# A two-layer attention and ternary-FFN kernel on one core: FFN statistics a step later, small work moved between engines, and the last output products reordered

## What is computed

```python
xn = layernorm(x)
x = x + attention(xn) + ffn(xn)
```

## Time and profile before

| | us |
|---|---|
| median of 3 runs | 380.17 (379.9 to 381.06) |
| the profiled execution | 380.05 |
| its span, first to last instruction | 378.2 |
| PE busy | 360.5 (95%) |
| DVE busy | 307.1 (81%) |
| POOL busy | 282.3 (75%) |
| ACT busy | 250.7 (66%) |

### The profile page before, as it was taken

The page is one execution under the profiler, slowest core; times in us unless marked ns, Lnnn a source line. Parts: engine busy times, 40 slices in busy tenths (PEclk is TensorE's granted clock), DMA queues, the critical chain, the costliest instruction groups (busy, mean ns, idle before and its releaser), DMA issues.

```text
span 378.2 us, 8305 instructions
## 1 busy us (share of the span) xinstructions
PE 360.5 (95%) x2808; PEld 335.7 (89%) x2824; DVE 307.1 (81%) x684; ACT 250.7 (66%) x804; POOL 282.3 (75%) x242
## 2 busy tenths in 40 slices
PE   8999988997899999999999999999999999999995
PEld 3668878997898999999999999999999999998984
DVE  6868998866999987879878887887787878888882
ACT  1367865563987666777767586867666777767771
POOL 5537759789999999999779697777987977775000
PEclk9999999999999999999999999999999999999999
DMA  7997001523343445343345743343455433334100
GB/s 258 412 409 314 28 30 45 144 66 83 85 109 97 118 118 149 101 121 87 83 114 143 178 114 103 102 105 85 126 136 162 122 85 85 84 100 105 50 2 28
DMA packets 35371, 46.19 MB, mean 122 GB/s; under 512 B 4609, under 2 KB 27138, under 8 KB 34946
## 3 DMA queue, kind: packets, MB, share of 16 engines
q1 hardware_dynamic: 35184, 45.66, 41.8%
q10 hardware_dynamic: 146, 0.00, 0.0%
HBM read 13.14 MB, written 1.05 MB: 38 GB/s over the span
## 4 chain that ended last, share of the span: by engine, by line
PE 80%; DVE 11%; ACT 4%; DMA 2%; issue 2%; POOL 0%; SPq 0%
PE bank L1321 17%; PE bank L1033 13%; PE bank L1341 12%; PE bank L1229 12%; PE bank L1281 10%; PE bank L1188 3%; PE bank L1287 3%; PE bank L1284 2%; ACT bank L519 2%; PE bank L1164 2%; PE bank L1042 2%; DMA wq0T<-in_L_attn_w_qkv_dram 2%; PE bank L1245 2%; DVE neg_max L940 1%; PE bank L1050 1%
## 5 line engine op out<-in xcount | busy, mean ns | idle before, releaser
L519 ACT ACTIVATE bank<-bank,neg_max 128x256 f32<-128x256 f32 (+1 forms) x256 | 101.1, 396 | 10.5 <-DVE neg_max L940 10.3
L528 ACT ACTIVATE probT_hi<-bank 128x512 fp32r<-128x512 f32 x96 | 57.7, 602 | 65.0 <-PE bank L1033 64.9
L940 DVE TENSOR_REDUCE neg_max<-bank 128x2 f32<-128x512 f32 (+1 forms) x96 | 65.9, 687 | 23.6 <-PE bank L1287 13.2
L1321 PE MATMUL bank<-probT_hi,v 128*128 128x256 f32 x384 | 76.5, 295 | 0.7 <-DVE oT_lo L968 0.7
L956 DVE TENSOR_TENSOR prob<-bank,rsum 128x512 f32<-128x512 f32 x96 | 66.4, 691 | 3.3
L962 DVE TENSOR_TENSOR probT_lo<-bank,probT_hi 128x512 fp32r<-128x512 f32 x96 | 65.3, 681 | 0.5 <-ACT probT_hi L528 0.4
L681 POOL TENSOR_TENSOR rope_b<-turned,cst 128x512 f32<-128x512 f32 x36 | 46.9, 1302 | 22.1 <-DMA turned<-raw 22.1
L1281 PE MATMUL bank<-kT,qT 128*128 128x256 f32 (+1 forms) x384 | 62.6, 272 | 0.0
L1033 PE MATMUL bank<-cst,prob 128*128 128x128 f32 x384 | 57.9, 273 | 4.3 <-DVE prob L956 3.3
L1321 PEld LDWEIGHTS bank<-probT_hi,v 128*128 128x128 f32 x384 | 58.7, 189 | 3.6 <-issue 2.3
L1281 PEld LDWEIGHTS bank<-kT,qT 128*128 128x128 f32 x384 | 55.0, 191 | 0.0
(11 more groups left out here) (163 smaller groups left out, 781.7 us busy)
## 6 DMA issues: line engine op xcount, KB each, us to landing
turned<-raw SPq DMA_DIRECT2D x72, 128.0 KB, 2.0
qT<-q_hi SPq DMA_DIRECT2D x64, 128.0 KB, 2.4
qT<-split_lo SPq DMA_DIRECT2D x64, 128.0 KB, 2.4
wq0T<-in_L_attn_w_qkv_dram SPq DMA_DIRECT2D x4, 512.0 KB, 7.9
wout<-in_L_attn_w_out_dram SPq DMA_DIRECT2D x4, 512.0 KB, 12.7
nat_qkv<-in_L_attn_w_qkv_dram SPq DMA_DIRECT2D x2, 1024.0 KB, 20.4
nat_o<-in_L_attn_w_o_dram SPq DMA_DIRECT2D x1, 2048.0 KB, 21.1
kT<-split_hi SPq DMA_DIRECT2D x16, 128.0 KB, 2.4
```

The source lines that it names most:

```text
L519: ins = nc.scalar.activation(own, own, ACT.Exp, bias=neg_max[it % 2][:, first + j:first + j + 1], accum_out=sums[it % 2][:, first + j:firs ...
L528: nc.scalar.activation(probT[0][:, n % 4, :], bank[2 + n % 2][:, :], ACT.Copy).then_inc(t_hi, 1)
L940: dve.tensor_reduce(neg_max[n // UNITS % 2][:, unit_columns(n % UNITS)], score_bank(n)[:, :].rearrange("p (h k) -> p h k", h=heads), AX.X, ...
L1321: ins = pe.matmul(group_bank(), v[b % 2][:, DH * z:DH * z + P], p, start=m == 0, stop=m == last)
```

## The change

- **Layer 0.** `m_products(3)` on PE moves ahead of the wait for `prob0` and its transposes. The four `high_part` copies move from DVE to ACT, two before the exponential and two after the signs of `ffn0`.
- **Tokens of batches 0 and 1.** ACT writes only the even tile of `y1`, POOL the odd one, right after `batch_root` of that batch; `turn_tokens` waits for both.
- **DVE's small products.** In `stats1`, `hidden_scale` and `hidden_stats` a `tensor_tensor` or `scalar_tensor_tensor` of two SBUF inputs becomes a `tensor_scalar` of one column (one for each of the two tiles where there are two). `hidden_scale(0)` moves behind `tokens_lo(0)`.
- **FFN statistics.** `hidden_stats(0)` leaves its place before the loop. `hidden_stats(t)` now runs in step t+1 instead of step t, after `hidden_lo(t)` and ahead of `hidden_factors(t-1)`; for the last tile it runs after `ffn_add(6)`.
- **Signs of the projection.** Two instructions of half the size in ACT's step 1, one before `gelu(1)` and one after the fill's copy, instead of one at the end of step 0. `proj(0)` and `column_sums` wait for both.
- **`mean_part`** moves from DVE (one instruction, slots 6 to 13) to POOL (two instructions, after blocks 10, 12, ... 24).
- **The end.** Slot 97 makes only the e = 0 half of `project_out(15, 0)`. After the last slot come its e = 1 half, then the e = 0 half of `project_out(15, 1)`, then its e = 1 half into bank 6 instead of bank 5. DVE adds bank 5 to both halves, then bank 6 to half 1; SP stores half 0 after the first addition, half 1 after the second.

```diff
 # SP
             sp.wait_ge(out_added, B)
-            sp.dma_start(rows[:, B - 1, :, :], x[:, B - 1, :, :]).then_inc(stored, 16)
-            sp.wait_ge(stored, 16 * B)
+            sp.dma_start(rows[:, B - 1, 0, :], x[:, B - 1, 0, :]).then_inc(stored, 16)
+            sp.wait_ge(last_added, 1)
+            sp.dma_start(rows[:, B - 1, 1, :], x[:, B - 1, 1, :]).then_inc(stored, 16)
+            sp.wait_ge(stored, 16 * (B + 1))
...
 # ACT
             whole_x(2)
+            high_part(0)
+            high_part(1)
             act.wait_ge(e_in, 1)
...
             sign(0, nat_ffn0[:, :, :], ffn0T[:, :, :], tern0)
+            high_part(2)
+            high_part(3)
...
             def normal1(b):
                 act.wait_ge(nb_done, b + 1)
-                for t in (2 * b, 2 * b + 1):
-                    ins = nc.scalar.activation(y1[:, b, t % 2, :], x[:, b, t % 2, :], ACT.Identity, bias=tok[:, 3, t:t + 1],
-                                               scale=tok[:, 0, t:t + 1])
-                ins.then_inc(y1_done, 1)
+                t = 2 * b
+                nc.scalar.activation(y1[:, b, 0, :], x[:, b, 0, :], ACT.Identity, bias=tok[:, 3, t:t + 1],
+                                     scale=tok[:, 0, t:t + 1]).then_inc(y1_even, 1)
...
                 hidden_hi(step - 1, 1)
+                if step == 1:
+                    sign(2, nat_proj[:, 0:4, :], projT[:, 0:4, :], tern_proj)
                 if step < TILES:
                     gelu(step)
                 if step < B - 1:
                     tokens_hi(step + 1)
                 empty(FILLS_IN.get(step, ()))
-                if step == 0:
-                    sign(2, nat_proj[:, :, :], projT[:, :, :], tern_proj)
+                if step == 1:
+                    sign(2, nat_proj[:, 4:8, :], projT[:, 4:8, :], tern_proj)
...
 # POOL
             def normal1(b):
-                for t in (2 * b, 2 * b + 1):
+                for e in range(0 if b >= 2 else 1, 2):
...
             batch_root(0)
+            normal1(0)
             batch_root(1)
+            normal1(1)
...
+            def mean_part(t):
+                if t == 0:
+                    pool.wait_ge(wcol_done, 1)
+                pool.wait_ge(f_add, t + 1)
+                pool.wait_ge(f_norm, t + 1)
+                part, share = x[:, t // 2, t % 2, :], mean_out[:, :]
+                pool.tensor_scalar(share, wcol[:, :], ffac[:, t, 4:5], None, ALU.mult).then_inc(f_share, 1)
+                pool.wait_ge(f_share, t + 1)
+                pool.tensor_tensor(part, part, share, ALU.add).then_inc(f_mean, 1)
...
                 weights_lo(min(n + 6, len(W_UNITS)), min(n + 7, len(W_UNITS)))
+                if n >= 10 and n % 2 == 0 and n < 10 + 2 * TILES:
+                    mean_part((n - 10) // 2)
...
 # DVE
             def hidden_scale(b):
                 link(dve.reciprocal(f1[:, own], ms[:, own]))
-                link(dve.tensor_tensor(f1[:, own], f1[:, own], ms[:, own], ALU.mult))
-                dve.scalar_tensor_tensor(ffac[:, own, 0], c[:, own], wscale[:, 1:2], f1[:, own], ALU.mult, ALU.mult).then_inc(f_fac, 1)
+                for t in (2 * b, 2 * b + 1):
+                    ins = dve.tensor_scalar(f1[:, t:t + 1], f1[:, t:t + 1], ms[:, t:t + 1], None, ALU.mult)
+                link(ins)
+                for t in (2 * b, 2 * b + 1):
+                    ins = dve.tensor_scalar(ffac[:, t, 0:1], c[:, t:t + 1], wscale[:, 1:2], f1[:, t:t + 1], ALU.mult, ALU.mult)
+                ins.then_inc(f_fac, 1)
...
             stats1(1)
-            hidden_scale(0)
             add0(2)
             tokens_lo(0)
+            hidden_scale(0)
             add0(3)
...
             stats1(3)
-            hidden_stats(0)
             hidden_scale(1)
             for step in range(1, STEPS):
                 t = step - 1
...
                 if step in (1, 2):
                     tokens_lo(step + 1)
-                if step < TILES:
-                    hidden_stats(step)
+                if t < TILES - 1:
+                    hidden_stats(t)
                 if t >= 1:
                     hidden_factors(t - 1)
                     ffn_add(t - 1)
+                if t == TILES - 1:
+                    hidden_stats(t)
...
             def slot(n):
-                if 6 <= n < 6 + TILES:
-                    mean_part(n - 6)
...
             add_out(B - 1)
+            dve.wait_ge(out_last, 1)
+            dve.wait_ge(out_added, B)
+            dst = x[:, B - 1, 1, :]
+            dve.tensor_tensor(dst, dst, bank[BANK_LAST][:, DIM:2 * DIM], ALU.add).then_inc(last_added, 1)
...
 # PE
             def turn_tokens(b):
                 pe.wait_ge(y1_done, b + 1)
+                if b < 2:
+                    pe.wait_ge(y1_even, b + 1)
...
+            m_products(3)
             pe.wait_ge(prob0, 1)
...
-            m_products(3)
             ffn_0(0)
...
-                if it and u in (1, 5):
+                if it == ITS and u == 1:
+                    project_out(it - 1, 0, (0,))
+                elif it and u in (1, 5):
                     project_out(it - 1, u // 5)
...
-            project_out(ITS - 1, 1)
+            project_out(ITS - 1, 0, (1,))
+            project_out(ITS - 1, 1, (0,))
+            emptied(pe, FILL[-1])
+            project_out(ITS - 1, 1, (1,), BANK_LAST)
```

More of the change, by code:

```diff
@@ L435, in whole_x, with high_part @@
                 ins.then_inc(full_done, 1)
+            def high_part(b):
+                act.wait_ge(full_done, b + 1)
+                nc.scalar.activation(xT[0][:, :, SEQ * b:SEQ * b + SEQ],
+                                     yT_full[:, b, :].rearrange("p (k t) -> p k t", k=KC), ACT.Copy).then_inc(x_hi, 1)
             keys_x(0)
@@ L649, in normal1 @@
                 pool.wait_ge(nb_done, b + 1)
[L650 to L651 removed]
+                for e in range(0 if b >= 2 else 1, 2):
+                    t = 2 * b + e
+                    ins = pool.tensor_scalar(y1[:, b, e, :], x[:, b, e, :], tok[:, 0, t:t + 1], tok[:, 3, t:t + 1],
                                              ALU.mult, ALU.add)
@@ L833, in _ @@
             ins.then_inc(prob0, 1)
-            for b in range(1, B):
-                high_part(b)
             def weight_scale(n, ps):
@@ L859, in stats1 @@
                 link(dve.reciprocal(ms[:, own], r[:, own]))
-                link(dve.tensor_tensor(ms[:, own], ms[:, own], var[:, own], ALU.mult))
+                for t in (2 * b, 2 * b + 1):
+                    ins = dve.tensor_scalar(ms[:, t:t + 1], ms[:, t:t + 1], var[:, t:t + 1], None, ALU.mult)
+                link(ins)
                 dve.tensor_scalar(tok[:, 3, own], mean[:, own], -1.0, None, ALU.mult)
@@ L902, in hidden_stats @@
                 link(dve.reciprocal(ffac[:, t, 2:3], fv))
-                link(dve.tensor_tensor(ffac[:, t, 2:3], ffac[:, t, 2:3], fv, ALU.mult))
+                link(dve.tensor_scalar(ffac[:, t, 2:3], ffac[:, t, 2:3], fv, None, ALU.mult))
             def hidden_factors(t):
@@ L975, in add_out @@
                 dve.tensor_tensor(dst, dst, bank[BANK_OUT][:, :].rearrange("p (e n) -> p e n", e=2), ALU.add).then_inc(out_added, 1)
-            def mean_part(t):
-                if t == 0:
-                    dve.wait_ge(wcol_done, 1)
-                dve.wait_ge(f_add, t + 1)
-                part = x[:, t // 2, t % 2, :]
-                dve.scalar_tensor_tensor(part, wcol[:, :], ffac[:, t, 4:5], part, ALU.mult, ALU.add).then_inc(f_mean, 1)
             def slot(n):
-                if 6 <= n < 6 + TILES:
-                    mean_part(n - 6)
                 if n % (HKV * UNITS) == UNITS and n > HKV * UNITS:
@@ L1323, in heads_out, with project_out @@
                 ins.then_inc(pv_done, 1)
-            def project_out(it, half):
+            def project_out(it, half, parts=(0, 1), place=BANK_OUT):
                 b, g = of_batch(it)
@@ L1335, in project_out @@
                     pe.wait_ge(w_lo, W_AT["woT", 2 * g + half] + 1)
-                for e in range(2):
+                for e in parts:
                     for s, w in W:
                         for j in (2 * half, 2 * half + 1):
-                            first = g == 0 and half == 0 and e == 0 and (s, w) == (0, 0) and j == 0
+                            first = place == BANK_LAST or (g == 0 and half == 0 and e == 0)
+                            first = first and (s, w) == (0, 0) and j == 2 * half
                             final = g == HKV - 1 and half == 1 and e == 1 and (s, w) == (0, 1) and j == 3
-                            ins = pe.matmul(bank[BANK_OUT][:, DIM * e:DIM * e + DIM], oT[s][:, j, e:e + 2 * P - 1:2],
+                            ins = pe.matmul(bank[place][:, DIM * e:DIM * e + DIM], oT[s][:, j, e:e + 2 * P - 1:2],
                                             woT[w][:, 4 * g + j, :], start=first, stop=final, skip_group_check=True)
                 if g == HKV - 1 and half == 1:
-                    ins.then_inc(out_full, 1)
```

(1 more changed line is left out.)

19 lines of the change are left out of this document (10 added, 9 removed).

## The result

The kernel after takes 382.91 us (median of 5 runs, 382.55 to 383.49), the kernel before 380.16 us (5 runs, 379.79 to 381.06). The ratio is 1.0073, 95% interval 1.0059 to 1.0087: slower by more than the 0.3% set as the bound, and outside the range. The profiled execution has a span of 380.7 us against 378.2, at a granted clock of 0.995 against 0.999.

A forecast was written before the change was run, and what follows sets the result against it. PE sets the pace from 120 to 340 us, with POOL as full at 120 to 145 and behind. Front 0, mean products 0, end -0.5: 380.05 becomes 379.5 us, range 377.2 to 381.1.

The forecast's parts named there:

- rival 3: Block 9 lands later still through POOL's late root of tile 6: slot 21 later, 380.8 to 381.4 us; chance 0.10.
- Rival 4: The wait at slot 21 halves PE's clock for one slot, costing up to 2.85 us: 382.4 us; chance 0.05.
- rival 1: POOL isn't the bound: the front's 3.4 us arrive and PE's stalls in slots 6 to 13 shrink, 375.4 us; chance 0.18.
- Layer 0, 1.2 us earlier: Before fc(0): the 0.66 us gap goes and sharing y1 saves 0.55, so fc(0) starts 1.2 us earlier.
- DVE's stretch, 1.65 us beyond that: From tokens_lo(0) to tile 0's addition: fewer statistics and unheld small products, 2.8 us earlier including layer 0's 1.2.
- 1.0 us back: In DVE's stretch: hidden_scale, held 1.22 us instead of 0.22 behind POOL, gets 1.0 us back as one-column tensor_scalar.
- PE to step 8, 0.6 us out of the wait: Ahead of proj(6): DVE no longer waits for gelu(7), 0.6 us less; PE reaches the slots 3.4 us early.
- The request for the root of tile 6, 81.9: DVE asks POOL for this root at 81.9 instead of 79.27, so POOL starts it 2.6 us late.
- POOL's lateness: POOL 2.3 us late from 85.58 on, 1.0 at block 8 after 1.3 us come back from mean_part.
- Slot 21, 150.2: Block 9 lands at 150.0, slot 21 starts at 150.1 to 150.2; the front's gain becomes a 3 us wait.
- The mean products, 1.3 us: On POOL after block 10 and later: 1.3 us for two instructions, the other seven (9 us) fit in at 0.
- The end, 0.5: Last addition and store are half as large: 0.27 + 0.23 = 0.5 us less, between 0.27 and 0.7.

The follow-up runs named there:

- run 3: The changed kernel with POOL's order alone changed, each root of a hidden tile one piece of RoPE work later: 376.22 us, ratio 0.9896.
- run 12: The changed kernel with POOL's roots one piece of RoPE later and the mean's share back on DVE: 377.57 us, ratio 0.9924.
- run 11: The kernel before with two layer 0 edits alone (high parts on ACT, m_products(3) ahead of the transposes): 380.47 us, ratio 1.0002.
- run 5: The changed kernel with the high parts of x back on DVE: 383.49 us, ratio 1.0086.
- S: Part of the change: FFN statistics one step later, projection's signs in two halves; alone on the kernel before 383.99 us.
- run 4: The kernel before with only the FFN statistics one step later and the projection's signs in two halves: 383.99 us, ratio 1.0104.
- run 1: The changed kernel with the FFN statistics and the projection's signs back in their old places: 379.73 us, ratio 0.9988.
- run 6: The changed kernel with the mean's share back on DVE, one instruction instead of two on POOL: 385.3 us, ratio 1.0130.
- run 2: The changed kernel with fifteen idle products on PE ahead of slot 21's wait: 382.5 us, ratio 1.0063.
- run 7: The kernel before with the change of its end alone: 379.47 us, ratio 0.9986.
- run 9: The kernel before with POOL's order alone changed, each root one piece of RoPE later: 383.12 us, ratio 1.0073.
- run 10: The kernel before with FFN statistics one step later, signs in two halves, and POOL's roots one piece of RoPE later: 377.86 us, ratio 0.9930.

## Why the prediction was wrong, step by step

**The sign, and what decided.** Forecast 379.5; what came is rivals 3 and 4 in one, 0.15 of the chances together. The mechanism of the sum held: POOL is late by its roots, block 9 lands late, and slot 21 eats the front's gain. With POOL's order put right (run 3) the kernel takes 376.22, near rival 1's 375.4, though by other terms: PE is 2.1 us early after the FFN (93.07 for 95.17) and not 3.4, and the mean off DVE gives 1.3 (run 12) and not 0.8. What failed are terms of the sum, two of which were put at nothing: the clock, and the later mean products on POOL.

**Layer 0, 1.2 us earlier: measured none.** This is the first step that failed, as "DVE loses its copies, which ACT takes where it otherwise waits" and "the gap of 0.66 us ahead of the transposes goes". Counted from the start of PE's products `bank<-g,xrT`, `fc(0)` starts after 18.82 us before and 18.88 after. The gap went elsewhere, for two reasons. The first is what the copies do on ACT: they stand ahead of its table load, and they let POOL start sooner. Neither was counted. ACT's timeline of the kernel after, with L446 the copies of batches 2 and 3:

```profile
26.82 1.14 ACT L446 ACTIVATE xT_hi<-yT_full 128x512 fp32r<-128x512 f32 x2
27.97 1.28 ACT L466 ACT_TABLE_LOAD   x1
...
29.38 0.57 ACT L468 ACTIVATE probT<-bank 64x512 f32<-64x512 f32 x1
```

Before, the load ran at 25.50 and the copy of probT at 27.08. Only about 1.0 of the load's 2.47 us are the copies L446 ahead of it. The other 1.43 come from the exponential, which starts at 24.98 instead of 23.55: with the high parts early, POOL's low parts start at 22.05 instead of 24.72 and hold DVE's first two-input products, which take 0.76 and 1.44 us instead of 0.29 and 0.49. Run 11 has these two edits alone, and `fc(0)` 0.31 us later than before.

The second reason shows with the copies back on DVE (run 5). `attention_0(0)` then starts at 29.09, 0.8 us earlier than before, but the gap comes back as a longer wait for `y`. The row of the kernel before, then that of run 5:

```profile
36.30 0.66 PE L1033 MATMUL bank<-cst,y 128*128 128x128 f32 x4 [0.78 <-ACT y L473]
```

```profile
36.13 0.63 PE L1057 MATMUL bank<-cst,y 128*128 128x128 f32 x4 [1.33 <-POOL y L659]
```

DVE reaches its first addition only 0.3 us earlier (30.64 for 30.96), with no idle time ahead of it, and its chain from there to the request for the root takes 3.2 us for 2.6. So `fc(0)` gains 0.3 us and not 1.2. The prediction counts four gaps of PE in this part, all ended by DVE. That leaves out this one of 0.78 us, ended by ACT, and one of 0.65 us ahead of `fc(0)` itself (38.59). Time that is gained ahead of them is waited for there. Sharing `y1` was worth 0.25 us: the wait for it is 0.39 us after and 0.61 in run 11, `fc(0)` 18.88 and 19.13 us behind the products named above.

**DVE's stretch, 1.65 us beyond that: measured 1.18.** Right in kind: `proj(1)` at 57.16 and `fc(0)` unchanged. The runs split it. From `fc(0)` to `proj(1)` the kernel before takes 19.75 us, with S alone 17.82 (run 4), the kernel after 18.50, and the change without S 21.80 (run 1). So S alone gives 1.9 us where the sum had 2.2. The other edits of DVE cost 0.7 us beside S, where the sum had 0.55, and 2.0 us without it. Their "1.0 us back" was mis-sized: the group of `hidden_scale` that was held took 1.52 us before (51.90 to 53.42) and takes 0.95 after (51.23 to 52.18). The one-column `tensor_scalar` is not held by POOL, in line with the row that the prediction took over the Trainium skill. But it is also longer than a two-input form that isn't held. The tile `ffac` after:

```profile
L899 DVE TENSOR_SCALAR ffac<-tok,wscale x8: 265/270/274, 39.0 to 57.7; 128x1 f32<-128x1 f32 x8
```

against 221 to 1224 ns of the earlier trace rows. The skill's caution isn't empty: the two-column form (`tok<-mv`, L881) took 169 to 720 ns in run 5. The Trainium skill ("VectorE: DVE Perf Modes", What auto-detection actually checks) has an instruction with a single source use both ports if source and destination are in SBUF and their outermost dimensions other than one are both even or equal; the two-column rows agree with it. For a single column, which has no dimension other than one, that rule doesn't settle the case, and the rows do.

**PE to step 8, 0.6 us out of the wait: right.** The gap ahead of `proj(6)` is 1.00 us for 1.65, and `proj(6)` starts at 85.04 for 86.88.

**The request for the root of tile 6, 81.9: measured 83.47.** The 1.2 and the 0.5 of the two steps above, carried on. Rival 3 priced it up to 0.6 us late; it was 1.6. The bounds were set around this step alone, and it stands behind two others.

**POOL's lateness.** At the root of tile 6 (82.2 forecast, 83.77 measured), at tile 7's (2.3, measured 3.8), at block 8 (1.0, measured 2.5): the same 1.5 us each time. The 1.3 us that `mean_part` gives back is exact: blocks 5 to 7 take 130.99 - 107.83 = 23.16. Run 6 prices it without the move: block 8 is 1.6 us later.

**Slot 21, 150.2: measured 151.80,** 1.5 us again. Rival 3's point of decision, a lateness of 1.6 at block 8, was passed. PE came at 148.24 instead of 146.8. A smaller wait of 1.24 us at slot 6 (102.84) was not foreseen: block 3, whose q parts it needs, starts at 91.19, for 87.37 before.

**Rival 4, the clock.** A PE gap of 3.56 us is followed by a clock of 0.50, as it feared. The Trainium skill ("TensorE: Matmul & The Clock Gate", What's actually happening) has an idle PE fall to half clock until work releases it; the trace agrees. The price between slots 21 and 27 was 1.7 us; what of it reached the end was 0.4 (run 2). It had to be added to rival 3 and not set beside it: whoever forecasts a gap of 3 us has the clock in the same sum.

**The mean products, 1.3 us: measured 1.7 a pair** (155.22 to 156.92). That "the other seven (9 us) fit in: 0" failed as a step too: POOL, in the kernel after, has no wait from 150 us until 219.80. Run 2 shows the price there: with the clock held, PE waits 1.25 us for a q block at 224.00. With the mean on DVE (run 6) POOL does wait in that stretch, for ACT's copies at 186.57 and 195.16. The mean products alone were not run on the kernel before; moving the mean is a gain on balance (runs 6 and 12).

**The end, 0.5: measured 0.5** (run 7), 0.8 by the two profiles.

**Sum with the measured terms**, against 380.05: 1.6 + 1.7 - 0.8 = +2.5, so 382.55, the profiled execution's own time to 0.1. The sum closes by position in time; it doesn't say that the time without the fall of the clock would be 1.7 us lower, for run 2 takes 382.5. The failed terms of the front alone, 1.6 us on the forecast of 379.5, lead to 381.1, the upper end of the range. What takes the time out of it are the two things that were not in the sum: the clock behind a forecast gap of 3 us, and POOL's later lateness, which is waited for where the clock is held.

## What to carry to other kernels

When an instruction moves to a later step on the engine that asks for it, move it in the order of the engine that answers as well: an in-order queue waits at it, and everything behind it is late. Test the two together, because each alone can lose what the pair gains. Look also at what the freed queue now runs beside: in run 9 POOL, no longer waiting, held DVE's small products. And before a copy is given to an engine because that engine waits anyway, read what stands behind it in that engine's order, here a table load on the critical chain, and which other engine it lets start sooner.

## What the runs showed of the hardware

- The same kernel, with the same program, has more than one time by the clock: in run 1, six runs of 378.9 to 379.3 us at 0.999 or 1.000, six of 380.15 to 380.3 at 0.995; in the kernel before 37 and 14 of 51, about 1.2 us apart. The profiled one of the second kind in run 1 had a PE gap of 1.93 us with a clock of 0.55 behind it; a gap of 1.66 us in the kernel before had none in its profile. The length of the gap alone doesn't tell: in run 10 the clock is 0.55 and 0.60 from 38 to 42 us behind a gap of only 0.65 us at 38.18. Gaps of 3.56, 4.23 and 4.33 us were all followed by 0.50: after the first the clock is back in the third stretch of 2 us, after the second (run 6) the three stretches from 154 to 160 us all have 0.50, and after the third and longest (run 4) it is 0.50, then 0.81, then back.
- Fifteen idle products in the wait keep the clock at 1.00. They give back the 1.7 us locally and 0.4 us in all. Keeping PE busy is worth only what the next wait doesn't take.
- DVE instructions of two SBUF inputs and one column take 159 ns or up to 1081 ns (run 10's `ffac<-ffac,fmv`), by what POOL does beside them, and the form with a single SBUF tensor and a scalar of one column 212 to 216 in the kernels that use it: it is never held, and slower than the first where that isn't held either.
